# TensorE's two programs for the gated FFN, in an If and its Else, change places

## The chip, the cores and the metric

The kernel runs on one core of one Trainium2 chip. The metric is the device time of one execution in microseconds. It is measured several times, and the median of the runs counts.

## What is computed

Two residual steps on 2048 tokens (4 x 512) of 512 features, all in float32:

```python
x = x + tanh(g_xattn) * experts(layernorm(x), token_ids, ctx, ctx, ctx)
x = x + tanh(g_ffn) * ffn(layernorm(x))

# experts: each token has one of four experts, by its id; gate, up and down all use ctx[e] (512 x 512)
g = silu(einsum('bsd,fd->bsf', h, Wg[e])); u = einsum('bsd,fd->bsf', h, Wu[e])
y = einsum('bsf,df->bsd', g * u, Wd[e])

# ffn: 512 -> 1408 -> 512, weights ternary (-1, 0, 1), one scale for each output
g = einsum('th,ih->ti', xf, gate_w) * gate_s
u = einsum('th,ih->ti', xf, up_w) * up_s
out = einsum('ti,hi->th', silu(g) * u, down_w) * down_s
```

## The kernel before

Each engine has a program of its own, written out by hand, and the engines meet in semaphores. The kernel has three stages. First the routing: the tokens are sorted by expert into up to 19 tiles of 128 rows. Then the expert stage: for each tile a gather by GpSimd, a layer norm, two products of 512 x 512 on TensorE, and a scatter of the updated rows. When only 18 tiles are needed, the flag no_18 is 1 and TensorE takes a short way past the 19th (lines 1278 to 1288). The third stage is the gated FFN: four blocks of four tiles (512 tokens), and in each block eleven chunks of 128 of the 1408 inner features. For a chunk TensorE makes the gate product and the up product (inner_product, line 1302), ScalarE and VectorE make the hidden layer of them, and TensorE adds the chunk's share of the down product for the four tiles into four PSUM banks (down_tile, line 1309), one chunk later than gate and up.

Matmuls keep float32 accuracy by splitting each operand into a high part, rounded to the format that TensorE reads in one go, and the low rest. A product is then a sum of passes, each a pair (part of the weight, part of the data). The general FFN needs three passes, high x high, low weight x high, and high x low data. If the weights have no low part, as small whole numbers have none, two passes do. The kernel looks at the weights it got: ScalarE sums the low 16 bits of all of them in the expert stage, VectorE makes a flag of the sums, and TensorE reads it into a register (has_lo, line 1277) before the expert stage ends. TensorE has both versions of its FFN program in its instruction stream, each with a loop over the four blocks (line 1370) and a tail for the last two chunks of the last block, which are done as four halves of two tiles each (last_two_chunks, lines 1337 to 1366). The test at line 1387 picks one. Inside the program two smaller tests stand, at lines 1376 and 1378. The other engines have one program for both cases.

The first thing that second_mlp does is to wait for the hidden layer of the last expert tile (h_ready), which VectorE makes at line 846; then the loop's register is set at line 1370, and the first inner_chunk follows. After the FFN's program TensorE goes to the end of the kernel, where all engines drain and meet (line 91 of the helper that closes the block). SyncE waits for the last four stores at line 388 before that. At the kernel's start TensorE runs warm-up matmuls whose results are not used (keep_busy, line 1225).

Of the kernel before, what the change touches and what calls it, by code (L numbers as in the profile page):

```python
# [82 lines left out]
def build(nc, x, ids, ctxT, g_x, g_f, guT, dwT, gate_s, up_s, down_s, out):  # L83
# [7 lines left out]
    with ExitStack() as ctx:  # L91
# [1041 lines left out]
        def _(pe):  # L1133
# [143 lines left out]
            has_lo = pe.value_load(flag[0:1, 0:1], min_val=0, max_val=1)  # L1277
# [37 lines left out]
            def down_product(b, c, passes):  # L1315
                pe.wait_ge(S["hlo_ready"], STEPS + IC * b + c + 1)
                pe.wait_ge(S["down_lo"], c + 1)
                for u in range(BLOCK):
                    if c == 0:
                        pe.wait_ge(S["scaled"], BLOCK * b + u + 1)  # L1320
                    down_tile(c, u, passes)

            def inner_chunk(b, c, passes):
                n = STEPS + IC * b + c
                pe.wait_ge(S["silu_ready"], n)
                lo_ready = None
                if c == 0:
                    pe.wait_ge(S["xhi0_ready"], BLOCK)
                    pe.wait_ge(S["xhi_ready"], STEPS + BLOCK * b)
                    lo_ready = (S["xlo0_ready"], BLOCK), (S["xlo_ready"], STEPS + BLOCK * b)  # L1330
                inner_product(g_ps, b, 0, c, passes, lo_ready=lo_ready).then_inc(S["z_done"], 1)
                if c == 0:
                    pe.wait_ge(S["rows_ready"], STEPS)
                pe.wait_ge(S["h_ready"], n)
                inner_product(u_ps, b, KC, c, passes).then_inc(S["u_done"], 1)

            def last_two_chunks(passes):
                b, n = BLOCKS - 1, STEPS + IC * (BLOCKS - 1) + IC - 2

                def end_half(e):  # L1340

                    (c, i), before = ends[e], n + max(e - 1, 0)
                    pe.wait_ge(S["silu_ready"], before)
                    pe.wait_ge(S["h_ready"], before)
                    pair = slice(2 * i, 2 * i + 2)
                    inner_product(gate_ps(e % 2), b, 0, c, passes, pair).then_inc(S["z_done"], 1)
                    inner_product(up_ps(e % 2), b, KC, c, passes, pair).then_inc(S["u_done"], 1)

                pe.wait_ge(S["down_lo"], IC)
                end_half(0)  # L1350
                end_half(1)
                pe.wait_ge(S["hlo_ready"], n)
                for c in range(IC - 3, IC):
                    pe.wait_ge(S["hlo_ready"], n + c - (IC - 3))
                    for u in range(2):
                        down_tile(c, u, passes)
                end_half(2)
                end_half(3)
                for u in range(2, BLOCK):
                    down_tile(IC - 3, u, passes)  # L1360
                pe.wait_ge(S["hlo_ready"], n + 3)
                down_tile(IC - 2, 2, passes)
                pe.wait_ge(S["hlo_ready"], n + 4)
                down_tile(IC - 1, 2, passes)
                for c in (IC - 2, IC - 1):
                    down_tile(c, 3, passes)

            def second_mlp(passes):
                pe.wait_ge(S["h_ready"], STEPS)
                with pe.Fori(0, BLOCKS) as b:  # L1370
                    for c in range(IC - 2):
                        inner_chunk(b, c, passes)
                        if c:
                            down_product(b, c - 1, passes)
                        else:
                            with pe.If(b > 0):
                                down_product(b - 1, IC - 1, passes)
                    with pe.If(b < BLOCKS - 1):
                        inner_chunk(b, IC - 2, passes)
                        down_product(b, IC - 3, passes)  # L1380
                        inner_chunk(b, IC - 1, passes)
                        down_product(b, IC - 2, passes)
                last_two_chunks(passes)

            with pe.If(has_lo < 1):
                second_mlp([(0, 0), (0, 1)])
            with pe.Else():
                second_mlp([(0, 0), (1, 0), (0, 1)])  # L1390


# [28 lines left out]
```

## Time and profile before

| what | value |
|---|---|
| median of 3 runs | 385.06 us |
| lowest and highest run | 382.82 and 387.72 us |
| the profiled execution | 382.92 us |
| its span, first to last instruction | 380.8 us |
| granted TensorE clock over the span | 0.997 |
| TensorE matmuls busy | 362.9 us (95%) |
| VectorE busy | 247.7 us (65%) |
| ScalarE busy | 148.6 us (39%) |
| GpSimd busy | 95.4 us (25%) |

The time of the profiled execution is near the lowest of the three runs. It is 2.1 us more than its span, for what lies before the first and behind the last instruction. Register, branch and semaphore instructions are not counted as busy; they appear in the views of a line, with a q behind the engine's name, for its sequencer: PEldq is the sequencer that issues TensorE's weight loads and matmuls. The instructions themselves come to the engines by DMA queues of the kind "instruction".

### The profile page before, as it was taken

The page shows a single profiled execution, that of the slowest core. Times are in us where ns is not written, and L with a number is a line of the kernel's source. Part 1 is how long each engine was busy: PE and PEld are TensorE (multiplying, and loading weights), DVE is VectorE, ACT ScalarE, POOL GpSimd, SP SyncE. Part 2 cuts the span into 40 slices and gives each one's busy share as a digit, 9 for nine tenths or more (in the row PEclk, how much of TensorE's full clock was granted, in tenths as well). Part 3 has the DMA queues.
Part 4 walks back from the last instruction along what each step waited for, and adds up shares of the span by engine and source line. Part 5 has one row for each costly group of instructions (what it writes and reads, how often), then busy time and mean ns, then how long its engine had stood idle before and what let it go on. Part 6 is the DMA issues. An engine that isn't in the chain of part 4 may idle for free.

```text
span 380.8 us, 5551 instructions
## 1 busy us (share of the span) xinstructions
PE 362.9 (95%) x1688; PEld 296.5 (78%) x1688; DVE 247.7 (65%) x455; ACT 148.6 (39%) x266; POOL 95.4 (25%) x132
## 2 busy tenths in 40 slices
PE   3889998999999999999999999999999999999992
PEld 2477876888888778888888888888888888888891
DVE  6877858889987788779855256647256647322363
ACT  4466565666565545323322223332222332222220
POOL 8499344554541120001002110002201001200022
PEclk9999999999999999999999999999999999999998
DMA  6868767789774155322202422301322200200012
GB/s 225 273 225 301 271 194 243 201 286 294 229 260 141 57 184 150 116 83 74 66 0 83 141 68 70 83 0 55 130 80 88 68 23 28 83 0 0 0 40 75
DMA packets 29969, 47.49 MB, mean 125 GB/s; under 512 B 3056, under 2 KB 15344, under 8 KB 29952
## 3 DMA queue, kind: packets, MB, share of 16 engines
q1 hardware_dynamic: 25600, 32.93, 27.3%
q0 software_dynamic: 4352, 14.35, 11.1%
q8 instruction: 9, 0.15, 0.2%
q14 instruction: 8, 0.07, 0.1%
HBM read 31.64 MB, written 15.62 MB: 124 GB/s over the span
## 4 chain that ended last, share of the span: by engine, by line
PE 83%; DMA 6%; DVE 5%; issue 3%; POOL 1%; ACT 1%; SPq 0%; ACTq 0%; DVEq 0%; POOLq 0%
PE bank L1302 41%; PE bank L1309 20%; PE bank L1197 19%; PE bank L1212 2%; DMA wraw<-guT 2%; DMA rows<-x,gidx 2%; DMA turned_rows<-tmp 1%; DMA xq<-turned_rows 1%; PE bank L1166 1%; DVE rows L1079 0%; DMA ids_i<-ids 0%; DVE tmp L1072 0%; DVE xn L1072 0%; DVE bn L785 0%; DVE is_low L732 0%
## 5 line engine op out<-in xcount | busy, mean ns | idle before, releaser
L1302 PE MATMUL bank<-work,wgu 128*128 (+1 forms) x736 | 167.3, 380 | 0.1
L1302 PEld LDWEIGHTS bank<-work,wgu 128*128 128x128 f32 x736 | 133.9, 188 | 27.1 <-issue 0.5
L1197 PE MATMUL bank<-work,parts 128*128 (+1 forms) x432 | 105.7, 397 | 1.4 <-DVE far L857 1.0
L1197 PEld LDWEIGHTS bank<-work,parts 128*128 128x128 f32 x432 | 79.2, 188 | 19.0 <-issue 2.5
L1309 PE MATMUL bank<-work,hp 128*128 128x512 f32 x352 | 87.2, 390 | 0.2 <-DVE hp L1038 0.2
L1309 PEld LDWEIGHTS bank<-work,hp 128*128 128x128 f32 x352 | 65.7, 188 | 14.4 <-DVE hp L1038 0.6
L1019 DVE SCALAR_TENSOR_TENSOR sh<-bank,gs,sh 128x512 f32<-128x512 f32 x42 | 31.5, 750 | 56.4 <-PE bank L1302 55.2
L652 ACT ACTIVATE hp<-sh 128x512 fp32r<-128x512 f32 x42 | 26.6, 634 | 79.3 <-DVE sh L1019 79.3
L647 ACT ACTIVATE sh<-bank,gs 128x512 f32<-128x512 f32 x42 | 28.9, 689 | 72.5 <-PE bank L1302 71.7
L517 POOL DMA_INDIRECT out<-rows x16 | 16.2, 1011 | 128.2 <-DVE rows L1079 105.7
L446 POOL TENSOR_TENSOR rstd<-ve,half 128x1 f32<-128x1 f32 x31 | 17.5, 564 | 109.8 <-DVE ve L792 109.4
L1025 DVE TENSOR_TENSOR hp<-sh,hp 128x512 fp32r<-128x512 f32 x42 | 29.0, 691 | 22.4 <-ACT hp L652 22.4
L428 POOL DMA_INDIRECT x_rows<-rows,sidx x15 | 15.4, 1027 | 27.6 <-DVE rows L857 26.5
L552 ACT ACTIVATE parts<-bank 128x512 fp32r<-128x512 f32 x19 | 11.4, 599 | 22.4 <-PE bank L1212 20.2
L785 DVE BATCH_NORM_STATS2 bn<-rows 128x6 f32<-128x512 f32 (+1 forms) x27 | 18.1, 672 | 0.4 <-DMA rows<-x,gidx 0.4
L423 POOL DMA_INDIRECT rows<-x,gidx x15 | 16.8, 1119 | 3.8 <-issue 2.6
L846 DVE TENSOR_TENSOR sh<-bank,sh 128x512 f32<-128x512 f32 x19 | 13.1, 688 | 5.9 <-ACT sh L556 5.7
L556 ACT ACTIVATE sh<-bank 128x512 f32<-128x512 f32 x19 | 11.4, 598 | 12.2 <-PE bank L1197 8.6
L1062 DVE TENSOR_TENSOR work<-rows,work 128x512 f32 (+1 forms) x12 | 8.3, 693 | 9.7 <-ACT work L547 9.7
L865 DVE STREAM_TRANSPOSE xt<-xq 128x512 f32<-128x512 f32 x12 | 13.0, 1087 | 1.7 <-DMA xq<-turned_rows 1.7
L850 DVE TENSOR_TENSOR parts<-bank,parts 128x512 fp32r<-128x512 f32 x19 | 13.0, 684 | 1.7 <-ACT parts L552 1.4
L865 DVE STREAM_TRANSPOSE rows<-rows 128x512 f32<-128x512 f32 x12 | 13.4, 1118 | 0.0
(143 smaller groups left out, 282.9 us busy)
## 6 DMA issues: line engine op xcount, KB each, us to landing
wraw<-guT SPq DMA_DIRECT2D x8, 704.0 KB
rows<-x_rows SPq DMA_DIRECT2D x8, 528.0 KB
ctx_in<-ctxT SPq DMA_DIRECT2D x4, 1024.0 KB, 7.3
turned_rows<-tmp SPq DMA_DIRECT2D x12, 256.0 KB
xq<-turned_rows SPq DMA_DIRECT2D x12, 256.0 KB
turned_rows<-xn SPq DMA_DIRECT2D x12, 256.0 KB
rows<-turned_rows SPq DMA_DIRECT2D x12, 256.0 KB
checked<-dwT SPq DMA_DIRECT2D x11, 256.0 KB
```

Source lines behind the costliest of these rows:

```text
L423: pool.indirect_dma_start(ring_row(k), None, x, bass.IndirectOffsetOnAxis(ap=gidx[:, k:k + 1], axis=0))\
L446: pool.tensor_tensor(rstd[:, 0:1], ve[:, 0:1], half[:, :], ALU.pow)\
L517: pool.indirect_dma_start(out, bass.IndirectOffsetOnAxis(ap=token_of(b, t), axis=0), rows[:, row_slot(b, t), 0:D], None).then_inc(done, 16)
L647: act.activation(sh[:, :], g_ps[:, :], ACT.Silu, scale=gs[:, 0, c:c + 1])\
L652: act.activation(hslot(c)[:, 0, :], sh[:, :], ACT.Copy).then_inc(S["hhi_ready"], 1)
L785: dve.bn_stats(bn[:, 0, :], row).then_inc(S["bn_parts"], 1)
L865: dve.transpose(turned_x(expert).rearrange("p (h a g) -> p g h a", h=KC, g=QUADS), quarter_rows(expert).rearrange(order, g=QUADS, h=KC))\
L1019: dve.scalar_tensor_tensor(out=sh[:, :], in0=u_ps[:, :], scalar=gs[:, 1, c:c + 1], in1=sh[:, :], op0=ALU.mult, op1=ALU.mult).then_inc(S["h ...
L1025: dve.tensor_tensor(hslot(c)[:, 1, :], sh[:, :], hslot(c)[:, 0, :].bitcast(F32), ALU.subtract).then_inc(S["hlo_ready"], 1)
L1197: mm = pe.matmul(out_ps[:, :], part(s)[:, c * P:(c + 1) * P], ctx_w(e, c, w), start=n == 0, stop=n == last)
L1302: mm = pe.matmul(out_ps[:, tiles.start * P:tiles.stop * P], wgu[:, row + h, w, c * P:(c + 1) * P], moving, start=n == 0, stop=n == last)
L1309: mm = pe.matmul(acc_ps[u][:, :], hslot(c)[:, s, u * P:(u + 1) * P], down_w(c, w), start=c == 0 and n == 0, stop=c == IC - 1 and n == len( ...
```

## The change

TensorE's two FFN programs trade places, and the test is turned round, so that each still runs in the same case:

```diff
-            with pe.If(has_lo < 1):
+            with pe.If(has_lo > 0):
+                second_mlp([(0, 0), (1, 0), (0, 1)])
+            with pe.Else():
                 second_mlp([(0, 0), (0, 1)])
-            with pe.Else():
-                second_mlp([(0, 0), (1, 0), (0, 1)])
```

The body of an If stands in the instruction stream right behind its test, and the body of its Else behind that. The If's body ends with a jump over the Else; the Else's body runs on into what follows.

## Rows read from the trace of the kernel before

**Rows 1.** The page: TensorE's total and slices, and the two FFN groups of matmuls.

```profile
PE 362.9 (95%) x1688; PEld 296.5 (78%) x1688; DVE 247.7 (65%) x455; ACT 148.6 (39%) x266; POOL 95.4 (25%) x132
...
PE   3889998999999999999999999999999999999992
...
L1302 PE MATMUL bank<-work,wgu 128*128 (+1 forms) x736 | 167.3, 380 | 0.1
...
L1309 PE MATMUL bank<-work,hp 128*128 128x512 f32 x352 | 87.2, 390 | 0.2 <-DVE hp L1038 0.2
```

**Rows 2.** Chain that ended last: start us, duration us, what.

```profile
132.95 0.12 issue
133.07 7.71 PE bank L1302 x32
...
186.22 3.63 PE bank L1302 x16
189.85 1.81 PE bank L1309 x8
191.66 3.63 PE bank L1302 x16
```

**Rows 3.** Windows: stretch, length, busy us of each engine, clock, DMA.

```profile
133.10:360.10 227.00, 227.00 (x1000) 187.63 (x1001) 131.27 (x206) 68.97 (x108) 21.11 (x26) 1.00 0.22 70
```

**Rows 4.** By line, windows 130:132, 372:373, 130:131: ns min/median/max, first, last start.

```profile
L1387 PEldq COMPARE_BRANCH  x1: 77/77/77, 130.8 to 130.8; - x1
...
L1387 PEldq COMPARE_BRANCH  x1: 3304/3304/3304, 372.3 to 372.3; - x1
...
L1278 PEldq COMPARE_BRANCH  x1: 316/316/316, 130.5 to 130.5; - x1
```

**Rows 5.** By line, whole span: the FFN loop's back edge.

```profile
L1370 PEldq COMPARE_BRANCH  x4: 67/210/213, 187.6 to 356.5; - x4
```

**Rows 6.** DMA in 373.2:374.3 (40 slices; queue row), then line 91 by line.

```profile
DMA  0090000000000000000000000000000000000000
...
q8 instruction: 1, 0.02, 5.2%
...
L91 PEldq DRAIN  x1: 64/64/64, 375.7 to 375.7; - x1
```

**Rows 7.** DMA in 131.4:133.1, 150.2:152.2, 177.7:178.8 and 178.8:368.5.

```profile
q8 instruction: 1, 0.02, 5.8%
...
DMA  0090009999995366537998996464510100102000
...
DMA  0000900000000000000000000000000000000000
...
q0 software_dynamic: 960, 3.15, 4.3%
q14 instruction: 2, 0.02, 0.0%
```

**Rows 8.** By line, 131:132.3 and 132:134; then the timeline of weight loads, 132.5:134.

```profile
L846 DVE TENSOR_TENSOR sh<-bank,sh x1: 682/682/682, 131.5 to 131.5; 128x512 f32<-128x512 f32 x1
...
L1370 PEldq MOVE  x1: 29/29/29, 132.2 to 132.2; - x1
...
133.06 0.99 PEld L1302 LDWEIGHTS bank<-work,wgu 128*128 128x128 f32 x5 [0.54 <-issue]
```

**Rows 9.** By line, SyncE's wait for the last stores.

```profile
L388 SPq EVENT_SEMAPHORE  x2: 28/4441/8854, 371.4 to 380.3; - x2
```

**Rows 10.** Windows as in rows 3, then the warm-up line in 9:13 and 13.2:15.5.

```profile
374.00:378.50 4.50, 0.00 (x0) 0.00 (x0) 1.75 (x3) 0.00 (x0) 1.92 (x2) 1.00 0.30 114
378.50:379.00 0.50, 0.00 (x0) 0.00 (x0) 0.00 (x0) 0.00 (x0) 0.00 (x0) 0.56 0.07 25
...
L1225 PE MATMUL bank<-minus_j,ones x8: 607/631/631, 9.8 to 12.8; 128*128 128x512 f16 x8
...
L1225 PE MATMUL bank<-minus_j,ones x6: 379/380/631, 12.8 to 15.2; 128*128 128x512 f16 x6
```

## The prediction

> **What bounds the kernel now.** I read the totals and the row of slices first, then the chain of waits, then TensorE's sequencer around the place of the change. TensorE is busy for 95% of the span and for nine tenths or more of nearly every slice, and the matmuls of the two FFN lines stood idle for 0.3 us in all [rows 1]. From 133.07 us on the chain of waits goes from matmul to matmul of these two lines, each piece starting where the one before it ends [rows 2]. In the 227 us from 133.1 to 360.1 TensorE is busy for 227.0 us, at full granted clock [rows 3]. So whatever TensorE loses between the expert stage and the first FFN matmul arrives at the end undiminished: there is no later pause that could swallow it. The tail behind that is a hand-over between TensorE, ScalarE and VectorE for the last half chunks, and then the last store and its landing.
>
> **What the diff changes, and what it leaves.** Which of the two programs runs is settled by the data. The FFN weights are ternary, so their low 16 bits are zero and has_lo is 0. The run shows it as well. The two-pass program has per block 11 chunks x (16 + 8) = 264 matmuls, the three-pass one 396, and the line of the inner products counts 736 matmuls, not over a thousand [rows 1]: four blocks of 11 x 16 = 704, plus 32, because the last two chunks are done as four halves of 16 matmuls. After the change the condition has_lo > 0 is false, so the same two-pass program runs, from the Else. No matmul, wait, buffer, transfer of data or instruction of another engine differs. What differs is where those instructions lie in TensorE's stream: now right behind the branch, then with the three-pass program between. That program is 396 matmuls in its loop, 96 in the four end halves and 36 in the end's down tiles, 528 in all, and each counts as two instructions (a weight load and a matmul, as the equal counts in [rows 1] show): over 1,056 instructions to jump over. The test has the same form, one compare and branch on a register.
>
> **What a branch costs TensorE, by the rows.** The sequencer is a resource of its own here, ahead of the array. The test of line 1387 is entered at 130.8 us and falls through to the two-pass program in 77 ns [rows 4]. The back edge of the FFN loop, taken three times, costs 0.21 us, and 0.07 us when it is not taken [rows 5]. One branch is in another class: at the end of the two-pass program, line 1387 jumps over the whole three-pass program to the kernel's end and takes 3,304 ns [rows 4]. In its time exactly one packet moves on the instruction queue, 0.02 MB, from about 373.25 us, 5.2% x 16 x 1.1 us = 0.92 us long, and TensorE's drain, the next thing at its target, starts at 375.7 us [rows 6]. This is an instruction fetch on demand: some 0.95 us to ask, 0.92 us to move, 1.4 us until the next instruction goes. The row fits the new case closely, since the jump I have to price crosses the same 1,056 and more instructions, from their head to their tail, on the same engine. I take 3.3 us for it as its bare price.
>
> How far ahead has the sequencer loaded? The instruction queue moves packets at 150.3 and 177.8 us (each is the first slice with a digit in [rows 7]): 27.5 us apart, 5.05 chunks of 3.63 + 1.81 = 5.44 us [rows 2], at 48 instructions each for matmuls and loads plus a few, so some 250 instructions to a packet. The jump therefore spans more than four packets. The one at 372.3 us shows that a target so far ahead is not there.
>
> **Where the 3.3 us fall.** Part is covered. In the kernel before, the sequencer has passed the branch by 130.9 us and then waits for the hidden layer: VectorE's last product of the expert stage starts at 131.5 and lasts 0.68 us, and the loop's first register move follows at 132.2 us [rows 8]. From there 0.84 us of setting up lead to the first FFN weight load at 133.06 us; the chain shows 0.12 us in which the array waits for that, behind its last expert matmul [rows 2, 8]. The new branch starts at the same 130.8 us and ends at 134.1 us. The wait is then long fulfilled, the same 0.84 us follow, and the first matmul moves by 134.1 - 132.2 = 1.9 us. That is the lower bound of the forecast.
>
> On top comes a collision. The jump over the other Else (line 1278) just before, at 130.5 us, takes 0.32 us, and behind it a packet of instructions starts right after 131.4 us and lasts 5.8% x 16 x 1.7 us = 1.6 us, so till 133.0 us [rows 4, 7]. It is the block that follows in order, which the new kernel does not need. The packet that it does need would be asked for so that it starts 0.95 us after 130.8, at 131.8 us. If it runs beside the other nothing is added. If it queues behind it, it starts at 133.0 us, 1.2 us later. If it also takes 1.6 us instead of 0.9, 0.7 us more. This gives 1.9, 3.1 and 3.8 us. I take 3.1: a queue that carries one packet after another is the plainest reading, and no rows show two instruction packets of TensorE at once. The worst bound for a miss: the request goes out only when the first packet is wholly dealt with, 133.0 + 1.4 = 134.4 us, then 3.3 + 0.7 us to 138.4 us, a shift of 6.2 us.
>
> **What else moves.** The end: after the change the two-pass program falls out of the If without the 3.3 us jump. TensorE drains at 375.7 us today, but SyncE waits for the last store until 380.3 us [rows 6, 9], so this gives back nothing. The loop's back edges: the head would again be within three packets of the loop's end, and in the 190 us from 178.8 to 368.5 us, with three turns of the loop, the rows list no packet on queue q8 (the last two of the three queues listed stand in [rows 7]): the loop stays loaded. Should a turn miss after all, the first one branches at 187.6 us and the array starts the next block's first chunk at 191.66 us [rows 2, 5]; a branch of 3.3 us ends at 190.9 us, and 0.84 us of setting up make it 191.7. Three misses cost 0 to 1 us together, 2 to 3 if each also takes the longer 1.6 us packet. Crossing from packet to packet inside the program is hidden now, with no idle array at 150 or 178 us [rows 3, 7], and should stay so: the second packet after the jump would come by about 138 us, and the sequencer needs it in the third chunk, after 141 us. Tiles, semaphores and the other four queues keep their order; their work behind the FFN's start moves with TensorE.
>
> **Weighed against the skill.** The rows show two prices, 0.07 to 0.32 us and 3.3 us [rows 4, 5]. The Trainium skill, Advanced Engine Details and Errata, Control Flow Timing, gives a compare and branch about 108 ns; by it the change would vanish in the 1.3 us between the branch and the end of the wait. The row at 372.3 us speaks against that for a far target. The Trainium skill, Runtime: NRT & Kernel Launch, Instruction fetch mechanics, says that a taken branch out of the current two-block window stalls for a fetch, which that row bears out; its same section gives TensorE an instruction memory of 2,048 instructions, and if so much lay ready ahead, the target would be there. That is the first rival.
>
> **Rivals.** (a) The jump costs nothing that shows: the target is loaded, or the build puts the executed program next to the branch after all, so that the change does not do what it says. Then the branch takes 0.1 to 0.3 us, inside 1.3 us of slack: 385.1 us. For it: all jumps but one are cheap. Against: the one that crosses the same distance is the dear one. (b) The request waits for the wrong packet to be finished, as worked out above: +6.2 us, 391.3 us. For it: the order of 130.5, 130.8 and 131.4 us; against: nothing shows that a request waits so. (c) The slower side, over 2%: the same, and TensorE's clock falls in the gap. The array would stand idle from 133.0 to 139.2 us. After its last matmul, which is over by 374.0 us, the granted clock is 1.00 until 378.5 us and half of it soon after [rows 10], so an idle time of 3 us has not cost the clock there and one of 6 us would. The price: at the start eight warm-up matmuls ran 631 ns long against 380 for those after them [rows 10], start to start 0.43 us against 0.22, over some 3.5 us from 9.8 us, so half of 3.5 us is lost: +1.8 us, 8.0 in all, 393.1 us. It decides from an idle time of some 4.5 us on, a shift of 4.6 us.
>
> **How the numbers follow.** The profiled execution took 382.92 us, with a span of 380.8 and 2.1 us around it; the forecast for such a one is 382.9 + 3.1 = 386.0 us. The median of the runs shown is 385.06 us, 2.1 above the profiled one, and the runs spread from 382.82 to 387.72 us. I add to the median: 388.1 us. Chances: the forecast (1.9 to 3.8 us, 387.0 to 388.9 us) 0.65; (a) 0.14; (b) without the clock 0.12; (c) 0.07; 0.02 for anything unforeseen. The range takes in (a), the forecast's bounds and (b), with some of the spread of the runs: 384.3 to 391.8 us. Within 2% (7.7 us), which is about what a measurement of this kernel can tell from no change, lie all cases but (c); with the spread of the runs: faster 0.02, same 0.90, slower 0.08.
>
> **What would show it.** Right: line 1387 has one compare and branch at 130.8 us of 3.3 to 5 us in place of 77 ns, and none of 3.3 us at the end; two instruction packets between 131 and 135 us, or one late; the first matmul of line 1302 at 135.0 to 136.9 us, with everything before it in place and the 227 us behind it as long as before; the end of the span later by the same amount. Wrong: a branch below 1.4 us (rival a), an idle array of over 4.5 us with a half clock behind it (c), long branches on line 1370, or new idle time in the middle of the FFN.

## The result and the profile after

| | before | after |
|---|---|---|
| median of 20 runs each | 384.75 us | 387.91 us |
| lowest and highest | 381.69, 387.92 us | 385.36, 391.72 us |
| profiled execution, its span | 382.92, 380.8 us | 387.93, 385.8 us |

The ratio is 1.0091, with a 95% interval of 1.0064 to 1.0118: the kernel is 0.9% slower, 3.2 us by the medians and 3.5 us (2.5 to 4.5) by the ratio, which leaves out runs over 1.5% above the fastest of the same kernel. The forecast was +3.1 us. As the rest shows, the total came out near while three of its terms did not: the stall was longer, and a loss of clock and a gain at the end were missing.

The page of the kernel after, against [rows 1]: TensorE's busy time went up by 2.6 us although it does the same 1,688 matmuls, and the first FFN line now shows 3.8 us of idle time in front of it. In the row of the clock one slice is below nine tenths, the one that begins at 135 us.

```profile
span 385.8 us, 5550 instructions
...
PE 365.5 (95%) x1688; PEld 298.6 (77%) x1688; DVE 247.4 (64%) x455; ACT 148.5 (38%) x266; POOL 95.4 (25%) x132
...
PEclk9999999999999969999999999999999999999999
...
L1302 PE MATMUL bank<-work,wgu 128*128 (+1 forms) x736 | 169.9, 384 | 3.8 <-issue 3.8
```

The chain of waits of the kernel after (start, duration, what), against [rows 2]. Before, 0.12 us of "issue" stood between the expert stage's last matmul and the first of the FFN; now it is 3.76 us. The first 32 FFN matmuls then take 10.36 us for 7.71.

```profile
130.13 2.95 PE bank L1197 x12
133.08 3.76 issue
136.84 10.36 PE bank L1302 x32
...
382.48 0.96 POOL out L517
```

The views of the lines 1387, 1278 and 1370 of the kernel after, against [rows 4, 5, 8]. There is one branch at 1387 instead of two, it is the long one, and the loop's first register move follows on its end. The back edges cost what they did.

```profile
L1387 PEldq COMPARE_BRANCH  x1: 5011/5011/5011, 131.0 to 131.0; - x1
...
L1278 PEldq COMPARE_BRANCH  x2: 77/202/328, 129.5 to 130.6; - x2
...
L1370 PEldq MOVE  x1: 29/29/29, 136.1 to 136.1; - x1
...
L1370 PEldq COMPARE_BRANCH  x4: 67/214/217, 194.0 to 362.8; - x4
```

The DMA view of 131.5 to 132.6 us of the kernel after, against [rows 7]: two packets of instructions, not one. They start in the slices with 596 GB/s (16 KB in a slice of 0.0275 us), the 3rd and the 37th of 40, so 0.9 us apart, and take 18.7% x 16 x 1.1 us = 3.3 us together, 1.6 to 1.7 each in the trace.

```profile
GB/s 0 0 596 0 0 0 0 0 154 768 154 461 461 154 307 614 154 461 461 307 307 461 154 461 614 307 307 461 154 461 461 307 154 0 0 0 596 0 0 0
...
q8 instruction: 2, 0.03, 18.7%
```

The windows of the kernel after (stretch, length, busy times, clock, DMA), against [rows 3, 10]: no matmul from 133.1 to 136.8 us, a clock that falls to half at 136.0 us, 2.9 us after the last matmul's end, and 6 us of matmuls at half rate. From 142.9 us on the FFN runs as it did.

```profile
133.10:136.00 2.90, 0.00 (x0) 0.00 (x0) 2.88 (x4) 0.60 (x1) 0.99 (x2) 1.00 0.06 7
136.00:136.80 0.80, 0.00 (x0) 0.00 (x0) 0.26 (x1) 0.00 (x0) 0.80 (x1) 0.50 0.91 312
136.80:142.80 6.00, 5.96 (x14) 4.71 (x15) 0.00 (x0) 0.69 (x1) 0.29 (x1) 0.50 0.56 182
142.90:363.90 221.00, 221.00 (x976) 182.81 (x975) 127.34 (x200) 67.18 (x105) 18.97 (x24) 1.00 0.21 66
```

And the end. First the kernel before: the last two stores of line 517, how long they take to land, and the DMA view of 376 to 378.2 us with the instruction queue; then the same stores of the kernel after.

```profile
L517 POOL DMA_INDIRECT out<-rows x2: 962/962/962, 374.7 to 376.1; - x2
...
DMA to landing us min/median/max: 4.1/4.5/4.9
```

```profile
DMA  0000198995977975200000000000099599799999
...
q8 instruction: 1, 0.02, 5.2%
```

```profile
L517 POOL DMA_INDIRECT out<-rows x2: 962/962/962, 381.1 to 382.5; - x2
...
DMA to landing us min/median/max: 2.7/2.7/2.7
```

Before, the last store landed 4.1 us after its issue, after the change 2.7 us. In the first case one more instruction packet moved meanwhile (by the order of the stream, the block behind the far jump's target), 5.2% x 16 x 2.2 us = 1.8 us on one DMA engine while the store was moving on nearly all of them, and the DMA view of 378.5 to 380.3 us shows what fits one engine still at work on the store's rest, packet after packet (9 packets of 4.3% x 16 x 1.8 us / 9 = 0.14 us, starting every third or fourth slice of 0.045 us, so one after the other):

```profile
DMA  0300002000200200020020002000000000000000
```

These rows add up to the 5.0 us between the two spans: 0.13 us that the expert stage ended later, 3.76 - 0.12 = 3.64 us of stall, 10.36 - 7.71 = 2.65 us of half clock, and at the end (385.8 - 382.48) - (380.8 - 376.06) = 3.32 - 4.74 = -1.42 us.

### The profile page after: what moved, and what is told of

It is laid out like the page before. It is cut to its first block, busy times and chain, and to the rows that moved or that the text cites. A ratio compares the mean times of both kernels' runs of the same rounds, so it can differ in the third digit from the quotient of the medians.

```text
span 385.8 us, 5550 instructions
## 1 busy us (share of the span) xinstructions
PE 365.5 (95%) x1688; PEld 298.6 (77%) x1688; DVE 247.4 (64%) x455; ACT 148.5 (38%) x266; POOL 95.4 (25%) x132
## 4 chain that ended last, share of the span: by engine, by line
PE 84%; DMA 6%; issue 3%; DVE 3%; POOL 2%; ACT 1%; SPq 0%; ACTq 0%; DVEq 0%; POOLq 0%
PE bank L1302 41%; PE bank L1309 20%; PE bank L1197 20%; DMA ctx_in<-ctxT 2%; PE bank L1212 2%; DMA turned_rows<-tmp 2%; DMA wraw<-guT 1%; DMA rows<-x,gidx 1%; DMA xq<-turned_rows 1%; POOL minus_j L406 1%; PE bank L1166 0%; DVE rows L1079 0%; POOL far L456 0%; DVE tmp L1072 0%; DVE sh L846 0%
## 5 line engine op out<-in xcount | busy, mean ns | idle before, releaser
L1302 PE MATMUL bank<-work,wgu 128*128 (+1 forms) x736 | 169.9, 384 | 3.8 <-issue 3.8
L1302 PEld LDWEIGHTS bank<-work,wgu 128*128 128x128 f32 x736 | 136.0, 191 | 31.3 <-issue 4.2
```

Of the source, the lines that this page charges most:

```text
L1302: mm = pe.matmul(out_ps[:, tiles.start * P:tiles.stop * P], wgu[:, row + h, w, c * P:(c + 1) * P], moving, start=n == 0, stop=n == last)
```

## The experiments

Theory: F, the fetch on demand at the far jump, made worse by a packet in flight (Q); C, the clock falls in the gap and costs more; T, the old kernel's far jump at the end delayed the last store, and this is given back. Rivals: a layout of the code that slows the FFN; a branch that costs as such; a slow packet without Q; a landing that differs by chance. The first four runs share a chip and 29 runs of the kernel before (median 383.52 us), if_next to hint 17 (384.62 us), hint_moved to hint_early 29 (383.56 us), and exit_hint has 17 of its own (383.96 us).

**after_again.** The changed kernel, unedited.

> The changed kernel once more, for a second trace. Theory F (a fetch on demand at line 1387, 5.0 us in the first trace): the branch takes 4.5 to 5.3 us again, the array stands idle for 3.4 to 4.0 us before the first FFN matmul, the last store lands 2.7 us after its issue (4.1 us before the change). Whether the clock falls in the gap (theory C: it does in some executions, not in all, and costs 2.6 us when it does) is open: the first 32 FFN matmuls take 10.4 us with it and 7.7 us without. Ratio to before 1.006 to 1.012. Rival (the layout of the code slows the FFN everywhere): idle time or longer chunks in the middle of the FFN.

Measured: ratio 1.0116 (1.0053 to 1.0179). The branch takes 5.48 us. The chain and two windows:

```profile
132.24 4.29 issue
136.53 9.16 PE bank L1302 x32
```

```profile
132.30:136.50 4.20, 0.00 (x0) 0.00 (x0) 3.12 (x4) 0.58 (x1) 1.88 (x2) 1.00 0.22 74
136.50:140.00 3.50, 3.47 (x8) 2.83 (x9) 0.00 (x0) 0.00 (x0) 0.04 (x1) 0.51 0.66 226
```

F holds, both numbers a little above what I gave. Here the clock was still full after 4.2 us without a matmul, and was at half for the next 3.4 us, which cost 9.16 - 7.71 = 1.45 us; in the first trace it fell after 2.9 us. The length of the pause alone does not tell when and for how long it falls.

Each run comes with the mean granted clock of its span, and 2 x (1 - clock) x span is its time at half rate, the idle end included. It is 8.5 us on the mean of the 20 runs of the kernel after and 8.0 us in these six, but 5.1 us in the 29 runs of the kernel before beside them (standard errors 0.6, 1.2 and 0.6 us). So the change adds about 3 us at half rate to a mean run. The idle end holds less of it than before: 2.2 us of the span in the traces of before and before_moved, 0.6, 2.0 and 1.3 us in those of after, after_again and after_moved. The start of the FFN then has about 4 us of it, and by 2.65 us for 6 and 1.45 us for 3.4 such microseconds that is an estimate of 1.8 us of time.

All seven traces with a pause of 2.2 to 4.3 us ahead of the FFN agree: the first 32 matmuls took 9.1 to 10.4 us in every one, 1.8 us more than 7.71 on the mean. In the seven with a pause of 0.86 us or less the clock stayed full there. So "in some executions, not in all" is not what the traces show: it fell in each of these seven.

**tail_short.** The end alone.

```diff
             with pe.If(has_lo < 1):
                 second_mlp([(0, 0), (0, 1)])
             with pe.Else():
-                second_mlp([(0, 0), (1, 0), (0, 1)])
+                pe.wait_ge(S["h_ready"], STEPS)
```

> The kernel before, with the three-pass program in the Else replaced by a single wait (left out: the case of weights with a low part, which these inputs do not reach). The If's closing jump then lands in the block that is loaded. Theory T (the jump over the three-pass program costs time at the end as well: the instruction packet that follows it occupies one DMA engine for 1.8 us while the last store goes out): the jump takes 0.1 to 0.3 us instead of 3.3, no instruction packet moves behind 370 us but the one of 368.6, the last store lands 2.7 to 2.9 us after its issue instead of 4.1, and the kernel takes 1.4 us less than before, ratio 0.996 to 0.997. Rival (the landing time differs by chance, as predicted: nothing is given back): ratio 1.000.

Measured: ratio 0.9964 (0.9925 to 1.0002). By line, the branch and the jump of 1387, then the last two stores:

```profile
L1387 PEldq COMPARE_BRANCH  x2: 77/128/179, 132.4 to 374.2; - x2
```

```profile
DMA to landing us min/median/max: 2.7/2.7/2.7
```

The jump is cheap over a short distance, no instruction packet moves from 370.5 us on, and the store lands in 2.7 us. The traces show T; the interval just reaches 1, so the time alone would not.

**if_short.** The changed order with a short If.

```diff
             with pe.If(has_lo > 0):
-                second_mlp([(0, 0), (1, 0), (0, 1)])
+                for _ in range(10):
+                    pe.transpose(bank[6][:, 0:P], ident[:, :], ident[:, :])
             with pe.Else():
                 second_mlp([(0, 0), (0, 1)])
```

> The changed kernel with the three-pass program in the If replaced by ten transposes, 21 instructions that are never executed (left out: the case of weights with a low part). Theory F (the distance is what costs): the taken branch at line 1387 takes 0.1 to 0.35 us, the first FFN matmul comes at 133.1 us as before, no clock loss; with theory T 1.4 us less than before, ratio 0.996 to 0.997. Rival (the Else side, or a branch that is taken, costs by itself): a branch of over 1 us and a ratio over 1.003.

Measured: ratio 0.9990 (0.9959 to 1.0021); TensorE was idle for 0.05 us ahead of the FFN.

```profile
L1387 PEldq COMPARE_BRANCH  x1: 223/223/223, 132.9 to 132.9; - x1
```

The Else and the taken branch cost nothing that shows (0.22 us, covered by the wait): the distance is what costs. Of the 1.4 us at the end less shows in the ratio than I expected, within its interval; the last stores land in 2.7 us here too.

**after_moved.** The block boundary moved away from the branch.

```diff
+            with pe.If(no_18 < 1):
+                for _ in range(90):
+                    pe.transpose(bank[6][:, 0:P], ident[:, :], ident[:, :])
             first_product(17, e_17)
```

> The changed kernel with 181 never executed instructions (90 transposes in an If that is false here) ahead of the 18th tile's step, so that the crossing into a new instruction block, and with it the unwanted packet, comes some 6 to 9 us before line 1387 and not 0.2 us before it. Theory Q (the unwanted packet in front makes the demanded one late, as the forecast took it): the branch takes 3.3 to 3.9 us, not 5.0, the array is idle for 2.0 to 2.7 us, ratio 1.003 to 1.007. Rival (the branch is long because its own packet is slow beside the other transfers of that moment): still 4.6 to 5.2 us.

Measured: ratio 1.0092 (1.0056 to 1.0128), above what I gave. The branch (line 1390 here), and the chain:

```profile
L1390 PEldq COMPARE_BRANCH  x1: 3790/3790/3790, 133.9 to 133.9; - x1
```

```profile
136.14 2.43 issue
138.57 9.15 PE bank L1305 x32
```

The branch is 1.2 us shorter than in the first trace and 1.7 us shorter than in the second: the unwanted packet does cost that, as Q says. But even a gap of 2.43 us had a half clock behind it (9.15 us for 32 matmuls), so less of it is saved than the stall says. In the time no saving shows: 1.0092 lies above my range for Q, and its interval overlaps that of after_again (1.0053 to 1.0179).

**if_next and if_two_on.** As if_short, with 160 and with 300 transposes.

> The changed kernel with the three-pass program in the If replaced by 160 transposes that are never executed, 321 instructions (left out: the case of weights with a low part). The branch at line 1387 then lands in the next block, the one whose packet starts just after the branch in every trace so far. Theory W (what lies ahead is the current block and the next): the branch waits for that one packet alone, from 0.9 us to the packet's start, 0.9 to 1.7 us of moving and 1.4 us, so 2.5 to 4 us in all, and no second packet is asked for before it ends. Rival (everything up to the instruction memory's size is there): below 0.4 us.

> The same with 300 transposes, 601 instructions: the target lies in the block after the next. Theory W: two packets side by side and a branch of 4.5 to 5.5 us, as with 1,111 instructions between; the distance beyond one block does not matter. Rival (loaded further ahead than one block): below 0.4 us, or as short as with 321 instructions.

Measured, one execution each: 386.08 and 390.06 us. Only their traces are read. The branch in the one and in the other:

```profile
L1387 PEldq COMPARE_BRANCH  x1: 3432/3432/3432, 131.7 to 131.7; - x1
```

```profile
L1387 PEldq COMPARE_BRANCH  x1: 5475/5475/5475, 132.7 to 132.7; - x1
```

A target one block ahead costs the rest of that block's fetch (one packet moves, at 132.9 us), one two blocks ahead as much as one over four blocks ahead (5.0 and 5.5 us; two packets again, at 133.3 and 134.2 us). What is ready ahead is the current block and, once its packet has come, the next. The "everything is there" rival is gone.

**after_fill.** Work in the gap.

```diff
+            for _ in range(4):
+                pe.matmul(bank[6][:, :], ident[:, :], dsb[:, :], start=True, stop=True)
             with pe.If(has_lo > 0):
```

> The changed kernel with four float32 matmuls of the identity with a full tile put between the expert stage and line 1387; their result is not used. They fill the gap in which the array waits for the instruction fetch. Theory C (part of what the change costs is TensorE's clock, which falls in that gap in some executions): the fetch stays at about 5 us and the first FFN matmul at its place or up to 0.3 us later, but the clock stays at 1.00 behind it, the first 32 matmuls take 7.7 us, and the mean over the runs falls by 1 to 2.6 us against the changed kernel: ratio to before 1.003 to 1.007. Rival (the clock falls as often with work in the gap, or has no part in it): ratio 1.009 to 1.012.

Measured: ratio 1.0102 (1.0060 to 1.0145), six runs. The branch, the chain and the windows:

```profile
L1389 PEldq COMPARE_BRANCH  x1: 5471/5471/5471, 135.2 to 135.2; - x1
```

```profile
137.25 3.43 PE bank L1388 x8
140.69 0.86 issue
141.55 7.58 PE bank L1302 x32
```

```profile
137.00:141.60 4.60, 3.74 (x11) 1.44 (x9) 3.14 (x4) 0.60 (x1) 1.92 (x2) 1.00 0.24 76
141.60:149.20 7.60, 7.60 (x33) 6.17 (x34) 3.59 (x5) 3.46 (x6) 0.00 (x0) 1.00 0.43 133
```

With a fetch as long as in after_again the clock stays full and the 32 matmuls take 7.58 us. The mean time at half rate over the six runs is 4.6 us, as before the change (5.0 in the runs beside them). That bears out C as far as the clock goes. The gain in time does not show: the ratio lies above the range that I gave for C and inside that of the rival. Its interval is 3.3 us wide, so six runs cannot tell a gain of 1.8 us, and what the clock costs in time rests on the rows of the traces.

**hint.** A fetch ahead of the branch. The If is written out, with the two-pass program as the taken target:

```diff
             expert_step(16, first=1)
+            ahead = pe.mark_branch_hint_location()
...
-            with pe.If(has_lo > 0):
-                second_mlp([(0, 0), (1, 0), (0, 1)])
-            with pe.Else():
-                second_mlp([(0, 0), (0, 1)])
+            pe.br_lt(pe.to_reg(has_lo), 1, on_true=two, on_false=three).branch_hint(ahead)
+            with nc.body(three, valid_engines=[pe.engine]):
+                second_mlp([(0, 0), (1, 0), (0, 1)])
+                pe.br(done)
+            with nc.body(two, valid_engines=[pe.engine]):
+                second_mlp([(0, 0), (0, 1)])
+                pe.br(done)
+            nc.switch_bb(done)
```

> The changed kernel's order, with the test written as a compare and branch that carries a prefetch hint, placed behind the 17th tile's step some 8 us ahead of line 1387 and naming the two-pass program as the likely target; the three-pass program is complete. If the fetch can be made ahead (theory F with T): one more instruction packet around 122 to 125 us, the branch takes 0.2 to 0.5 us, the first FFN matmul at its old place, no clock loss, and the end without the packet that delays the last store: 1.4 us less than before the change, ratio 0.995 to 0.998, which beats both kernels. Rival (the hint is dropped, or the crossing into the next block pushes the hinted one out): the branch still takes 3.3 to 5 us and the ratio is 1.006 to 1.012.

Measured: ratio 1.0034 (0.9992 to 1.0076).

```profile
L1389 PEldq COMPARE_BRANCH  x1: 3743/3743/3743, 131.3 to 131.3; - x1
```

```profile
133.34 2.60 issue
135.94 9.14 PE bank L1303 x32
```

The hint runs at 121.0 us, and no packet moves on q8 from there to 130.8 us. Then, at the crossing just ahead of the branch, a single packet moves, where the kernel after has two, and the branch waits for it. The trace does not name the block that a packet carries; the plainest reading is that the hinted block was asked for at the crossing, in place of the next one, and hint_moved tests it. My expectation of a fetch of its own at 122 us was wrong, and the ratio lies between my two ranges. The trace has a shorter stall than the kernel after, 2.60 us for 3.76, with the half clock still behind it. In the time the gain is not shown: the interval overlaps that of after_fill beside it.

**hint_moved.** Hint and padding together.

> The changed order with the prefetch hint behind the 17th tile's step and the 181 never executed instructions between the hint and line 1387; the three-pass program is complete. In the first try with a hint no packet followed the hint itself; the one packet came after the next crossing into a new block, and it was the hinted one. Theory H (a hint changes what the next crossing fetches, it fetches nothing by itself): the crossing now comes at about 127.5 us, one packet moves at 128 us, the branch takes 0.2 to 0.5 us, the first FFN matmul follows the last expert matmul by 0.1 to 0.3 us, and the end is without the packet behind the last store. Then the kernel takes 1 to 1.5 us less than before the change, ratio 0.995 to 0.999. Rival (the hinted block is dropped before it is used): 3.3 us or more at the branch and a ratio over 1.004.

Measured: 382.62 us, ratio 0.9975 (0.9938 to 1.0012). The branch (line 1392), the chain, and the landing of the last three stores (2.9 us is the last one's):

```profile
L1392 PEldq COMPARE_BRANCH  x1: 480/480/480, 136.0 to 136.0; - x1
```

```profile
138.20 0.12 issue
138.32 7.71 PE bank L1306 x32
```

```profile
DMA to landing us min/median/max: 2.7/2.9/3.5
```

The stall is gone, 0.12 us as before the change, and so is the half clock behind it. One packet moves at 130.4 us, none between it and the end of the branch at 136.5 us, and the far target was there: that packet was the hinted block. The profiled execution of this kernel, and that of exit_hint, lost 6.8 us of full clock at 60 us, well ahead of the FFN; only such local rows are read from them.

**before_moved.** The padding alone, on the kernel before.

> The kernel before with the same 181 never executed instructions, without a hint: what the padding costs and whether the place of the block boundaries matters in the FFN. Theory F: nothing but the skipped If, 0 to 0.3 us; the loop now lies over four blocks instead of three and still turns without a packet; one far jump at the end of 3.3 us; the last store lands 4.1 us after its issue or, if the packet behind the jump meets another DMA engine's work, less. Ratio 1.000 to 1.002. Rival (a loop over four blocks does not stay loaded): packets in every turn and idle array time.

Measured: ratio 1.0010 (0.9974 to 1.0045).

```profile
L1390 PEldq COMPARE_BRANCH  x2: 77/1929/3781, 132.7 to 375.3; - x2
```

The landing of the last two stores:

```profile
DMA to landing us min/median/max: 2.7/3.3/3.8
```

The padding costs nothing that shows, a loop over four blocks turns without a packet on q8 (none from 190 to 370 us), and the far jump at the end is back, with a late last landing (3.8 us). Here the store before the last landed in 2.7 us and the instruction packet came at 380.1 us, 1.1 us after the last store was issued.

**hint_early.** The hint one tile earlier, ahead of the crossing at 118 us, without padding.

> The changed order with the hint one tile earlier, ahead of the 17th tile's step, and no padding; the three-pass program is complete. The crossing that follows the hint is then the one at about 118.5 us. Theory H: the packet at 119 us is the hinted one. If the next block in order is fetched as well, the branch takes 0.2 to 0.5 us and the ratio is 0.995 to 0.999. If it takes the place of the next block, the crossing at line 1278 (0.32 us so far) becomes the long one, about 3.3 us or more, with the branch at line 1387 short, and the ratio is 1.004 to 1.010.

Measured: ratio 1.0021 (0.9974 to 1.0067).

```profile
L1389 PEldq COMPARE_BRANCH  x1: 3443/3443/3443, 130.0 to 130.0; - x1
```

Neither of my two cases. The hint ran at 114.2 us, the crossing at 117 us fetched the next block as ever (the jump at the Else before the branch took 0.36 us), and the hinted block came again only with the crossing just ahead of the branch. The three kernels with a hint so far agree on one reading: the hinted block is fetched when the sequencer enters the block that holds the hinted branch.

**exit_hint.** The order of before, with a hint for the jump that leaves the two-pass program.

```diff
+                exit_ = pe.mark_branch_hint_location() if hint else None
                 last_two_chunks(passes)
...
+            with nc.body(two, valid_engines=[pe.engine]):
+                exit_ = second_mlp([(0, 0), (0, 1)], hint=True)
+                pe.br(done).branch_hint(exit_)
```

> The order of the kernel before (two-pass program next to the test), complete, with a prefetch hint ahead of the last two chunks for the jump that leaves the two-pass program. Theory T with the rule that the three tries with a hint agree on (the hinted block is fetched when the sequencer enters the block that holds the hinted branch, in place of the next one): the packet at about 368.6 us is the target's, the jump takes 0.2 to 0.5 us instead of 3.3, the packet behind it moves at about 373 to 374.5 us and not beside the last store, which lands 2.7 to 2.9 us after its issue instead of 4.1. Head as before: 77 ns at line 1387, no idle array. 1 to 1.4 us less than before, ratio 0.995 to 0.999. Rival (the packet has no part in the late landing): it lands 4.1 us after its issue also with an early packet, ratio 1.000.

Measured: 382.13 us, ratio 0.9976 (0.9945 to 1.0007). The jump (line 1393), the landing of the last three stores (3.1 us is the last one's), and another instruction queue from 380.5 to 385.5 us:

```profile
L1393 PEldq COMPARE_BRANCH  x1: 426/426/426, 378.1 to 378.1; - x1
```

```profile
DMA to landing us min/median/max: 2.7/3.1/3.8
```

```profile
q14 instruction: 1, 0.01, 1.0%
```

The jump went from 3.3 to 0.43 us, and the packet behind it now runs ahead of the last store, which lands 3.1 us after its issue, not 2.7 to 2.9 as I expected; the one before it took 3.8 us. The likely reason lies in q14: in the ten kernels with a plain If its last packet moves 1.6 to 1.9 us behind the end of the span, and in the four with a written-out branch it moves at 379.1 to 382.2 us, beside the last stores, of which the last but one landed in 3.5 to 3.9 us and the last in 2.8 to 3.1. That this packet delays them as the one of q8 did before is argued from the order of time, not tested.

This kernel and hint_moved are complete, and their medians are 1.8 and 0.9 us below that of the kernel before; both intervals reach just past 1, so that either beats the kernel before is likely and not shown. Nor is all of that difference the fetch: the time outside the span is 1.7 us in all four kernels with a written-out branch and 2.2 in the runs of the kernel before beside them, so 0.4 us comes with the written-out form.

## Why the prediction was right, point by point

- **What bounds the kernel, and that nothing swallows a loss.** Right: from 142.9 us on 221 us are busy throughout. The sign "the 227 us behind it as long as before" did not hold: the first 32 matmuls took 2.65 us more.
- **The same program runs; only the place differs.** Right: 736 matmuls on line 1302.
- **A far jump costs 3.3 us.** Right as its bare price: 3.8 us without the unwanted packet (after_moved), its own packet taking longer there.
- **The collision.** Right in that there is one, wrong in how. I took 1.2 us, the demanded packet queuing behind the other. The two packets ran side by side (they start 0.9 us apart and take 3.3 us together). Against the 3.3 us jump, 0.5 us more passed until the demanded packet started (132.49 against the branch's 130.99), 0.7 us more while it moved (1.61 for 0.92, the term that I had worked out and not taken), and 0.5 us more behind it (1.9 for 1.4), for which the runs give no reason. The branch took 5.0 and 5.5 us, 1.2 to 1.7 us more than in after_moved; the stall came to 3.64 us more than before against 3.1 forecast, in the second trace to 4.2 us.
- **"This gives back nothing".** This step failed. I looked at who arrives last at the end, SyncE with the store, and not at what the far jump sets off: the packet behind its target delayed that very store. It gives back 1.4 us against that trace (in before_moved the last store landed in 3.8 us, so 1.1 there). The row was in the trace of before.
- **The clock as rival (c), deciding from an idle time of 4.5 us.** This step failed too. It fell after 2.9 us in one trace, was full for 4.2 us in the next, and a gap of 2.4 us had a half clock behind it. It is part of the likeliest case, at an estimate of 1.8 us on the mean, not a case of its own with a chance of 0.07. The price that I gave it, 1.8 us, was of the right size. I read the limit off one pause of the trace.
- **The sum.** 3.6 to 4.2 us of stall, 1.8 us of clock, 1.4 us given back: 4.0 to 4.6 us on the mean, where the medians say 3.2, the ratio 3.5 (2.5 to 4.5), and that of after_again 4.5. That the forecast of 3.1 us came so near is in part luck: the clock left out on one side and the gain at the end on the other nearly cancel. What it had by its mechanism is the stall, 3.1 of 3.6 to 4.2 us.
- **Rivals (a) and (b).** The jump was not free, and the figure of the Trainium skill (Advanced Engine Details and Errata, Control Flow Timing) for a compare and branch, about 108 ns, comes near only for targets that are loaded (0.07 to 0.48 us here). Nor did the request wait for the wrong packet to be dealt with (b), which would have been a branch of over 7 us. The two-block window of the Trainium skill (Runtime: NRT & Kernel Launch, Instruction fetch mechanics) is right ahead of the sequencer, as if_next and if_two_on show. Behind it more stays loaded: the loop over four blocks of before_moved turned without a fetch.

## What to carry to other kernels

Put the branch arm that usually runs right behind its test, and look where the arm's own exit jumps to: both a far Else and a far exit made TensorE fetch instructions on demand here, for 3.3 to 5.5 us. At the test its array stood idle for 2.4 to 4.3 us of them. Price a stall of TensorE with the clock that may fall behind it, and an instruction fetch with the DMA engine that it occupies: at the end of a kernel it can delay the last store though the engine that jumped is no longer needed. When a forecast comes out right, add up its parts from the trace all the same.

## What the runs showed of the hardware

- One 16 KB packet of instructions, 1.8 us on one DMA engine, put off the landing of a store that moves on nearly all of them by 1.4 us, from 2.7 to 4.1 us after its issue (before; without the packet 2.7 us in tail_short).
- Two instruction packets of TensorE run side by side. In all four traces that have such a pair (after, after_again, after_fill, if_two_on) the second starts 0.9 us behind the first and 1.5 us behind the start of the branch, where a branch with no other packet under way has its own after 0.9 to 1.0 us. The two take 1.6 to 2.4 us each, but single ones took up to 1.8 us beside other transfers and 0.9 us at the least, so how much of that is due to the pair is not shown.
- A prefetch hint fetches nothing when it is executed. In all four kernels that have one, a single packet moved when the sequencer entered the block with the hinted branch, and it was the hinted block in place of the next one (by hint_moved and exit_hint, where the branch then took 0.48 and 0.43 us). It removed the wait where that crossing lay some 4 to 6 us ahead of the branch (hint_moved, exit_hint), and a part of it where it lay right ahead (3.7 and 3.4 us).
- After TensorE stood idle for 2.2 to 4.3 us ahead of the FFN, its granted clock was at half for 3.4 or 6.8 us in all seven traces that have such a pause, and full in the seven with 0.86 us or less. At the end of the kernel before it stayed full for over 4.5 us after the last matmul [rows 10].
- The spread of the runs, 6 to 8 us from lowest to highest, is in good part the clock: over the 29 runs of the kernel before, the time goes up by about 0.6 us for each microsecond at half rate, which ranges from 1.5 to 11.6 us.
